# Per-sample weight mixing on one core: the weight table is spread by TensorE, the loops lose their peeled first turn, and ScalarE issues the stores

## What is computed

```python
w = weights[subjects]
out = jnp.einsum('bct,bcd->bdt', x, w)
x = x + out
```

## Time and profile before

| | |
|---|---|
| median of 3 runs | 330.95 us (330.91 to 331.18) |
| profiled execution | 331.55 us |
| its span, first to last instruction | 329.2 us |
| PE, DVE, ACT, POOL busy | 72%, 47%, 39%, 29% of the span |
| moved by DMA | 135.33 MB, mean 411 GB/s |

### The profile page before, as it was taken

How to read it: one execution, slowest core, us unless ns; L and a number is a source line. 1 busy time by engine, 2 the same in 40 slices (tenths; PEclk the granted TensorE clock), 3 DMA queues, 4 the chain that set the end, 5 groups by cost and what they waited for, 6 DMA issues and landing times.

```text
span 329.2 us, 4043 instructions
## 1 busy us (share of the span) xinstructions
PE 236.5 (72%) x1024; PEld 107.3 (33%) x1024; DVE 156.3 (47%) x128; ACT 129.9 (39%) x129; POOL 95.1 (29%) x136
## 2 busy tenths in 40 slices
PE   0599999877677687686686786776776876866800
PEld 0244444333233233233233242332332332332300
DVE  0057767645535535435445445345355354454420
ACT  1045656534424424424334334334244244344320
POOL 1634434422323313223223223223232233230000
PEclk9999999999999999999999999999999999999975
DMA  7999999999999999999999999999999999999992
GB/s 148 409 426 419 427 422 428 429 423 426 427 426 428 428 427 426 426 427 427 429 429 424 428 426 426 428 429 426 425 427 425 428 430 426 427 425 427 427 430 101
DMA packets 19495, 135.33 MB, mean 411 GB/s; under 512 B 2081, under 2 KB 3106, under 8 KB 3106
## 3 DMA queue, kind: packets, MB, share of 16 engines
q1 hardware_dynamic: 19488, 135.27, 98.5%
q10 hardware_dynamic: 2, 0.00, 0.0%
HBM read 68.16 MB, written 67.11 MB: 411 GB/s over the span
## 4 chain that ended last, share of the span: by engine, by line
PE 65%; DVE 15%; DMA 9%; ACT 4%; issue 2%; DVEq 1%; POOLq 0%; SPq 0%; POOL 0%; ACTq 0%
PE products L137 65%; DVE out_ring L158 15%; DMA x_ring<-x 6%; ACT out_ring L178 4%; DMA table<-weights 2%; DVEq L34 1%; POOLq L105 0%; POOL selected L112 0%; SPq L63 0%; SPq L73 0%; ACTq L176 0%; POOLq L112 0%; SPq L77 0%; DVEq L163 0%; POOLq L97 0%
## 5 line engine op out<-in xcount | busy, mean ns | idle before, releaser
L137 PE MATMUL products<-x_ring,selected 64*128 64x512 f32 x1024 | 236.5, 604 | 76.5 <-DVE out_ring L158 48.2
L158 DVE COPY out_ring<-products 64x1024 f32<-64x1024 f32 x128 | 156.3, 1221 | 159.2 <-PE products L137 157.2
L178 ACT COPY out_ring<-products 64x1024 f32<-64x1024 f32 x128 | 128.6, 1005 | 183.7 <-PE products L137 182.1
L137 PEld LDWEIGHTS products<-x_ring,selected 64*128 64x128 f32 x1024 | 107.3, 189 | 204.8 <-issue 107.5
L112 POOL TENSOR_TENSOR selected<-table,unit 64x256 f32<-64x256 f32 x128 | 93.7, 732 | 199.4 <-PE products L137 153.3
L178 ACT ACT_TABLE_LOAD x1 | 1.3, 1283 | 1.4 <-PEq L192 1.4
L93 POOL TENSOR_SCALAR_AFFINE_SELECT unit<-ones 64x256 f32<-64x256 f32 x2 | 0.8, 412 | 0.1
L88 POOL MEMSET ones<- 128x256 f32 x1 | 0.3, 311 | 0.3 <-POOLq L192 0.3
L192 POOL MEMSET const-float32-0.0<- 128x1 f32 x1 | 0.1, 99 | 0.1
L192 POOL MEMSET const-float32-1.0<- 128x1 f32 x1 | 0.1, 98 | 0.0
L192 POOL MEMSET const-bfloat16-1.0<- 128x1 bf16 x1 | 0.1, 98 | 0.0
## 6 DMA issues: line engine op xcount, KB each, us to landing
x_ring<-x SPq DMA_DIRECT2D x64, 1024.0 KB, 26.9
out<-out_ring SPq DMA_DIRECT2D x64, 1024.0 KB, 26.5
table<-weights SPq DMA_DIRECT2D x2, 512.0 KB, 6.5
subject_row<-subjects ACTq DMA_DIRECT2D x1, 0.5 KB
```

What stands on the lines that cost most here:

```text
L137: last = nc.tensor.matmul(products[:, b, g, n * BANK:(n + 1) * BANK], selected[part, k, e * mixed:(e + 1) * mixed], x_ring[part, s, e * ti ...
L158: nc.vector.tensor_copy(out_ring[0:HALF, s, b * times:(b + 1) * times], products[b * HALF:(b + 1) * HALF, s % PSUM_BUFS, 0, :]).then_inc(e ...
L178: nc.scalar.copy(out_ring[HALF:channels, s, b * times:(b + 1) * times], products[b * HALF:(b + 1) * HALF, s % PSUM_BUFS, 1, :]).then_inc(o ...
```

## The change

Four things change.

1. **The table.** The weights are loaded once, in their natural layout (`loaded`, 128 partitions x 8 subjects x 128 columns, 512 KB). TensorE multiplies them by a 0/1 matrix `spread`, which copies channel `2q+e` to partitions `q` and `64+q`, into PSUM: 4 matmuls of 512 columns over all 128 rows. VectorE adds the unit matrix in two operations, one for each parity `e`, and writes `table`. In doing so it puts the columns in the order in which the matmuls want them.
2. **The selection.** GpSimd copies the picked weights (`tensor_copy`) instead of adding the unit matrix.
3. **The loops.** TensorE's and GpSimd's loops have no first turn apart. The semaphores `even_drained`, `odd_drained` and `product_ready` start at a raised count instead. SyncE's last turn isn't apart either, as it no longer stores.
4. **The stores.** ScalarE issues the store of a tile behind its own two copies, and waits first for VectorE's. SyncE issues loads alone, and waits for the product of the tile (`product_ready`) instead of its copies. ScalarE waits for the last stores at the end.

```diff
-            for g in range(2):
-                sp.dma_start(table[g * HALF:(g + 1) * HALF], w_rows).then_inc(table_loaded, DMA)
+            sp.dma_start(loaded[:], weights.rearrange("n c d -> c n d")).then_inc(weights_loaded, DMA)
...
-                    sp.wait_ge(even_drained, 2 * tile + 2)
-                    sp.wait_ge(odd_drained, 2 * tile + 2)
-                    sp.dma_start(out_rows[bass.ds(tile * channels, channels), :],
-                                 out_ring[:, s]).then_inc(stored[s], DMA)
-                    if not last:
-
-                        sp.dma_start(x_ring[:, s], x_rows[bass.ds((tile + TILES_PER_TURN) * channels, channels), :]
-                                     ).then_inc(x_loaded[s], DMA)
...
+                    sp.wait_ge(product_ready, PRODUCT_FREE + tile + 1)
+                    sp.dma_start(x_ring[:, s], x_rows[bass.ds((tile + TILES_PER_TURN) * channels, channels), :]
+                                 ).then_inc(x_loaded[s], DMA)
...
+            nc.gpsimd.affine_select(spread[:], ones[:], [[-1, 2], [0, 2], [-2, HALF]],
+                                    ALU.is_equal, 0.0, base=0, channel_multiplier=1).then_inc(spread_ready, 1)
...
+                        nc.gpsimd.tensor_copy(selected[part, k:k + 1, :],
+                                              table[part, bass.ds(subject, 1), :]).then_inc(weights_selected, 1)
...
+            pe.sem_inc(product_ready, PRODUCT_FREE)
+            pe.wait_ge(spread_ready, 1)
+            pe.wait_ge(weights_loaded, DMA)
+            for e in range(2):
+                for n in range(banks):
+                    cols = slice(n * BANK, (n + 1) * BANK)
+                    last = nc.tensor.matmul(products[:, 0, e, cols], spread[:, e * channels:(e + 1) * channels],
+                                            loaded[:].rearrange("c n d -> c (n d)")[:, cols], start=True, stop=True)
+                last.then_inc(weights_spread, 1)
...
+            for e in range(2):
+                dve.wait_ge(weights_spread, e + 1)
+                nc.vector.tensor_tensor(
+                    table[:, :, e * mixed:(e + 1) * mixed].rearrange("p n (b m) -> p n m b", b=2),
+                    products[:, 0, e, :].rearrange("p (n m b) -> p n m b", n=n_subjects, b=2),
+                    unit[:, e * mixed:(e + 1) * mixed].rearrange("p (m b) -> p m b", b=2).unsqueeze(1).to_broadcast(
+                        [channels, n_subjects, HALF, 2]),
+                    ALU.add).then_inc(table_ready, 1)
...
+                    act.wait_ge(odd_drained, DRAINED_FREE + 2 * tile + 2)
+                    act.wait_ge(even_drained, DRAINED_FREE + 2 * tile + 2)
+                    act.dma_start(out_rows[bass.ds(tile * channels, channels), :],
+                                  out_ring[:, s]).then_inc(stored[s], DMA)
```

More of the change, by code:

```diff
@@ L89, in _ @@
             pool.wait_ge(ones_ready, 1)
+            nc.gpsimd.affine_select(spread[:], ones[:], [[-1, 2], [0, 2], [-2, HALF]],
+                                    ALU.is_equal, 0.0, base=0, channel_multiplier=1).then_inc(spread_ready, 1)
+            pool.wait_ge(spread_ready, 1)
             for g in range(2):
                 part = slice(g * HALF, (g + 1) * HALF)
-                nc.gpsimd.affine_select(unit[part, :], ones[part, :], [[128, 2], [-128, 2], [-1, HALF]],
-                                        ALU.is_equal, 0.0, base=0, channel_multiplier=1).then_inc(unit_ready, 1)
-            pool.wait_ge(unit_ready, 2)
+                if g:
+                    pool.wait_ge(unit_ready, g)
+                nc.gpsimd.affine_select(unit[part, :], ones[part, :], [[1, 2], [-1, mixed]],
+                                        ALU.is_equal, 0.0, base=0, channel_multiplier=2).then_inc(unit_ready, 1)
             pool.wait_ge(subjects_loaded, DMA)
-            pool.wait_ge(table_loaded, 2 * DMA)
-            def go_round(turn, first=False):
+            pool.wait_ge(table_ready, 2)
+            with pool.Fori(0, turns) as turn:
                 for s in range(TILES_PER_TURN):
@@ L106, in go_round @@
                                                   min_val=0, max_val=n_subjects - 1)
[L107 to L113, removed]
-                            unit[part, :].rearrange("p (e b m) -> p e b m", e=2, b=2),
-                            ALU.add).then_inc(weights_selected, 1)
-            go_round(0, first=True)
-            with pool.Fori(1, turns) as turn:
-                go_round(turn)
+                        if g == 0:
+                            pool.wait_ge(product_ready, PRODUCT_FREE + tile - SELECT_BUFS + 1)
+                        nc.gpsimd.tensor_copy(selected[part, k:k + 1, :],
+                                              table[part, bass.ds(subject, 1), :]).then_inc(weights_selected, 1)
         @block.tensor
         def _(pe):
-            def go_round(turn, first=False):
+            pe.sem_inc(product_ready, PRODUCT_FREE)
[7 more added lines that the diff above has]
+                last.then_inc(weights_spread, 1)
+            with pe.Fori(0, turns) as turn:
                 for s in range(TILES_PER_TURN):
@@ L128, in go_round @@
                     pe.wait_ge(weights_selected, 2 * tile + 2)
-                    if not first or s >= PSUM_BUFS:
-                        pe.wait_ge(even_drained, 2 * (tile - PSUM_BUFS) + 2)
-                        pe.wait_ge(odd_drained, 2 * (tile - PSUM_BUFS) + 2)
+                    pe.wait_ge(even_drained, DRAINED_FREE + 2 * (tile - PSUM_BUFS) + 2)
+                    pe.wait_ge(odd_drained, DRAINED_FREE + 2 * (tile - PSUM_BUFS) + 2)
                     for n in range(banks):
@@ L142, in go_round @@
                     last.then_inc(product_ready, 1)
-            go_round(0, first=True)
-            with pe.Fori(1, turns) as turn:
-                go_round(turn)
         @block.vector
         def _(dve):
+            dve.sem_inc(even_drained, DRAINED_FREE)
+            dve.wait_ge(unit_ready, 2)
+            for e in range(2):
[6 more added lines that the diff above has]
+                    ALU.add).then_inc(table_ready, 1)
             def go_round(turn, first=False):
@@ L152, in go_round @@
                     tile = turn * TILES_PER_TURN + s
[L153 removed]
+                    dve.wait_ge(product_ready, PRODUCT_FREE + tile + 1)
                     if not first:
@@ L184, in _ @@
                 go_round(turn)
+            for s in range(TILES_PER_TURN):
+                act.wait_ge(stored[s], turns * DMA)
 def kernel(x, itok_B_0_7, L0_cond_weights):
```

24 lines of the change are left out of this document (13 added, 11 removed).

## The result

The changed kernel takes 327.08 us (median of 4, 326.79 to 328.69), beside 330.94 us before. The ratio is 0.9891, with a 95% interval of 0.9877 to 0.9904: 3.9 us faster. I forecast 1.8. The profiled execution took 326.79 us with a span of 324.8, so it gained 4.4 us of span on the one before.

A forecast was written before the change was run, and what follows sets the result against it. The slowest DMA engine's pace was taken as the bound, with a head before the stream and a tail. Only the weight load counted, 1.8 us, all else 0: 330.95 - 1.8 = 329.15 us, range 326.0 to 332.4.

The forecast's parts named there:

- What bounds it: Whole kernel: a head of 8.1 us, a stream at the slowest DMA engine's 2.497 us per 1 MB transfer, a tail.
- The weight load: Ahead of the x stream on every DMA engine: half the bytes shorten the head, forecast gain 1.8 us.
- the middle between the second and the third: Weight load: the value taken, 1.8 us, between bounds of 1.0 and 2.6 us gained.
- a line through two packet sizes: Weight load: packet cost from 80 ns at 1 KB and 307 ns at 8 KB gives 64 ns, gaining 1.0 us.
- a rate of 204 GB/s that stays: Weight load: the old table's rate stays while the bytes halve, gaining 2.6 us.
- The highest value, 3.9: Weight load: us gained if the transfer, now filling all 128 partitions, runs at 427 GB/s.
- The way to the first product: Weights, spreading, additions, selection, first tile: product at 21.9 to 24.6 us, 4 to 6 later than 18.30; cost 0.
- The cover: Start: the 8 first loads last until 26.3 us, so the ninth must be issued by 24.3; cost 0.
- the rival of the late product: Start: first product outruns the loads; chance 0.07 that it eats the gain (331.3 us), 0.06 that it costs more.
- The loads' wait: SyncE's loads go out at the product, 2.5 us earlier than at the drained copies, not behind stores: gain 0.
- Stores on ScalarE: ScalarE's work with the store is 3.4 us of 4.99 per tile, the issue 0.37: cost 0.
- The rival of two queues that move the rate: DMA stream: load and store queues change the rate; up 0.11 chance, 326.0 us; down 0.15, 332.4 us.

The follow-up runs named there:

- e1: The kernel before with only the weight load exchanged for one 512 KB transfer over 128 partitions, spreading left out: 327.43 us against 331.22, ratio 0.9889.
- e4: The kernel before with the table's 1.05 MB in the same 1 KB packets, but one transfer over 128 partitions, bytes from x: 329.03 us, ratio 0.9937.
- e5: The kernel before with the table's 1.05 MB still in two transfers of 64 partitions, but in 8 KB packets from x: 330.56 us, ratio 0.9986.
- e3: The changed kernel with the stores and their waits back in SyncE's queue, each store ahead of its load: 329.06 us, ratio 0.9946 against the kernel before.
- e7: The changed kernel with the first spread matmuls run three times over, making the first product late: 329.90 us, ratio 0.9971 against the kernel before.
- e9: The changed kernel with each of the last two stores cut into 120 and 8 partitions: 332.09 us, ratio 1.0020 against the kernel before.
- e2: The kernel before with only the stores issued by ScalarE and the loads waiting for the product: 329.58 us, ratio 0.9947.
- e10: The kernel before with one natural 512 KB weight load, spreading left out, and the stores issued by ScalarE: 326.20 us, ratio 0.9854.
- e13: The changed kernel as it is, measured again on the same chip: 326.35 us, ratio 0.9852 against the kernel before.

## Why the prediction was wrong

**What bounds it: right.** Bytes over rate, with the slowest DMA engine as the pace, a head ahead of the stream and a tail behind it. The increments of the semaphores bear it out, with one share that falls 1.8 us behind in each 100 before. The rate was 427 GB/s in every kernel here between 40 and 300 us, and each gain or loss at the start could be read off the windows.

**The weight load: the term that failed, by its size.** I had four values for it, 0, 1.0, 2.6 and 3.9 us, and took 1.8, "the middle between the second and the third". It measured 3.8, by the windows of the changed kernel and by e1. The step that failed is this middle. It gave weight to a line through two packet sizes and to a rate of 204 GB/s that stays, and both leave out that the old transfers filled 64 partitions each. The ground for that stood beside it in the text: their windows looked like half of 427. e4 and e5 show that this was the cause. The line mixed a transfer over 64 partitions with one over 128, so its price per packet was no price per packet. Over 128 partitions the packets of 512 bytes, 1 KB and 8 KB took 27, 46 and 309 ns, a line of 8 ns and 0.037 ns a byte. The one that I drew had 47 ns and 0.032. Taking a middle between a mechanism that was true and one that wasn't gave a number that neither of them makes.

The highest value, 3.9, had the right mechanism, but it came out so near partly by luck. It took the new load to run at 427 GB/s, for 1.23 us. It ran at 303 by its packets, 64 packets for each engine at 27 ns, 1.7 us, and what made up for much of that is an earlier start: 0.10 MB had come by 3.0 us, where before it was 0.02.

The Trainium skill, in "DMA: Bandwidth & Descriptors", section "Specifications", puts the smallest transfer at full rate at 512 bytes. I held the 1 KB packets of before against it, and these had another cause. But the rule doesn't hold in full here either: packets of 512 bytes took 27 ns, 303 GB/s, where 8 KB packets make 424. "The descriptor swizzle" on the same page has partitions 0 to 63 on the even ports alone. The halved rate of e5 agrees with that; no run here shows the ports themselves.

**The way to the first product: 21.2, forecast 21.9 to 24.6.** The weights came two microseconds earlier than I took. The spread took 5.7 us, not 6.9, as its last three records stood 0.43 us apart and not 0.85 like the first. They have no partner in the other half of the array, so the 0.43 that I read off was not the work of pairs. The clock fits instead: the trace's first record of it begins at 9.42 us, at full level (2.4 GHz), where the spacing halves, and at 17.29 before, where it halves too. The windows print 1.00 ahead of it as well, where there is no record; 0.85 us apart is also what the records stand in the stretch of 16.25 to 19.66 us, at half level. The additions took 1.94 us each: between my 1.2 and 2.5, near the second. The 2.7 us to the first tile held, and the first tile took 5.4. The cover held too: I put the edge at an issue by 24.3, and with the head 2.0 us shorter than I took it, that is the 22.0 or so which e3, e7 and e9 bear out within half a microsecond. The margin of 0.7 us is thinner than "the queue grows" sounds. Two prices of the rival of the late product don't add up: with its 0.5 us for the first store a chain of 27.5 gives 332.9 and not 332.4, and the time turns slower from 26.3 on, not 26.8. The forecast doesn't use them.

**The loads' wait: I costed it at nothing, and together with the queue of its own it is worth 2.0 us here.** e3 shows it: with the old wait and the stores in the same queue, the late product cost the DMA engines 2.0 us of their rate. I named the 2.5 us by which the load goes out earlier and then dismissed them "while the DMA engines are busy anyway". At the start of the changed kernel they wouldn't have moved their full rate. e3 moves the stores back as well, so it doesn't price the wait by itself. The sum wasn't hurt by it, since the wait came with the change.

**Stores on ScalarE: right in form.** Issues took 0.33 to 0.39 us in the loops, the queue never filled by this, landings took 35.0 and 35.5 us where I wrote 36 and 34.

**The rival of two queues that move the rate: half right.** The mean rate didn't move. The slowest engine's backlog did in e2 and e10, which were 1.0 to 1.6 us faster for it. In the changed kernel itself it shows less: its first ratio, 0.9891, is no better than e1's 0.9889, while e13's, 0.9852, is as good as e10's. Between these two measurements of one kernel lie 0.8 us, so I can say that the head gives 3.8 and the second queue something between 0.1 and 0.9, and no closer.

**What stays open.** Which DMA engine is slow, why it falls behind by 4 to 6 us in 320, and why a second queue shortens that in some kernels and not in others. Also why some kernels vary more from run to run: the changed kernel and e2, with two queues, by 1.9 and 2.1 us, but e10, with two queues as well, by 0.6, and the kernel before by 1.0 at most.

## What to carry to other kernels

When DMA engines are busy throughout, look at the first ten microseconds in windows of one: here transfers that wrote only 64 of the 128 partitions moved at about half the rate, with packets of 1 KB as of 8 KB, and everything queued behind them was late by that. Where two mechanisms would explain a slow transfer and give different prices for the new one, ask which of them the rows of before already tell apart, rather than take a value between; a kernel like e4, which changes one line, tells them apart. And when work is added ahead of the first result, compute by when the next load must be issued to keep the DMA engines fed: here an edit that cost nothing was about 0.7 us away from costing.

## What the runs showed of the hardware

- Loads into 64 partitions ran at 188 to 254 GB/s from 4 us on, with packets of 1 KB (before) and of 8 KB (e5). At first, until 4 us, the 1 KB packets still took 46 ns.
- A packet of a load over 128 partitions took 27 ns at 512 bytes, 46 ns at 1 KB (e4) and 309 ns at 8 KB, by 16 engines 303, 356 and 424 GB/s. Over 64 partitions it took 84 ns at 1 KB and 605 ns at 8 KB.
- One of the 16 shares of each transfer falls behind steadily, whatever the kernel, and the last store's lands 4 to 6 us behind its eighth. Meanwhile 16 to 33 GB/s of traffic go on. The pace per tile in the second half of each kernel, 4.96 to 5.00 us for 2.1 MB, is that of the slow share (420 GB/s at 5.00), not of the mean 427.
- VectorE adding from PSUM in steps (128 x 1024 float32) took 1.94 us, a copy of as many elements per partition in order, over 64 partitions, 1.22. The two differ in the operation too.
- While stores cut into 120 and 8 partitions were under way (e9, 316 to 318 us), the rate was 311 GB/s; with whole ones it was 427.
